# Three recurrent layers and an attention: the scan's blocks of four rounds, five of them passes of one loop, become three blocks of 16, 16 and 4 rounds written out

## The chip, the cores and the metric

The kernel runs on one core of a Trainium2 chip, in float32. The metric is the time of one execution on the device in microseconds (us), as the median of three runs. TensorE does the matmuls, VectorE (DVE in the profile), ScalarE (ACT) and GpSimd (POOL) the elementwise work, SyncE (SP) issues transfers. Each engine runs its own stream of instructions; they meet at semaphores.

## The reference

The input x holds 8 sequences of 512 time steps and 512 features, cond is the first state of each. Three recurrent layers and one causal attention are each added to x in turn:

```
_L0: step(h, x_t):
        fused = sigmoid(concatenate([x_t, h]) @ w_W + w_b)
        hidden_state, output_state = split(fused, 2)
        memory_state = x_t @ wx_W + wx_b + hidden_state * (h @ wh_W + wh_b)
        h_new = output_state * h + (1.0 - output_state) * tanh(memory_state)
_L1, _L2: xw = x @ Wx + b
        step(h_prev, xw_t): h_next = tanh(xw_t + h_prev @ Wh)
_L3: causal multi-head attention (16 heads of 32) over x, with one more key and value from cond

x = x + _L0(x, cond)
x = x + _L1(x, cond)
x = x + _L2(x, cond)
x = x + _L3(x, cond)
```

The scans are serial in time: 512 steps, each with matmuls of an 8-row state with 512x512 weights. What does not hang on the state (x_t times a weight) can be computed for many time steps at once.

## The kernel before

All of x lies in SBUF as X. Time is cut into chunks of 16 steps (CH), 32 in all (NCH). The scan goes by rounds of 16 steps: in round m, layer 0 runs over chunk m, layer 1 over chunk m - 2 and layer 2 over chunk m - 4, so that all three run at the same time, shifted. With the shift there are 36 rounds (ROUNDS). From round 4 to round 31 all three layers run in each; rounds 0 and 1 hold layer 0 alone, and rounds 32 to 35 only the rest of layers 1 and 2.

One step of a full round, on TensorE: 16 matmuls (32 records in the trace) for the reset gate and the candidate of layer 0 (L181, into ps0), 16 for its update gate (L187), 16 for layers 1 and 2 together (L201, `main12`), and then the "fills": one or two groups of 16 matmuls (L225) that multiply a staged chunk with an input weight, for the steps of the next round. The 20 fills of a full round are spread over its 16 steps, two of them in every fourth step. VectorE turns the results (L328, L335 and L269), adds the input products, gates, and writes the new state h0 (L356); ScalarE does the sigmoids and tanh (L250, L253, L256, and L237, which writes the state h12). VectorE copies each finished fill out of PSUM with its bias (`keep_fills`, L290). Once a round and layer VectorE adds a finished chunk of states to X (L309), and GpSimd copies the next chunk of X to the staging tile of its layer (L381). `plan(m)` says what a round holds.

Within a block the streams are written out in full. `scan_rounds` makes one block of four rounds (PER_BLOCK): it calls `scan_block` and then `clear_signals`, a barrier of all engines that sets the semaphores to zero, so that a block counts from zero again. All waits in a block are for numbers counted from its start (`n0`, `n12`, `nfill`, `nchunk`). Before and after the streams of a block each engine branches (L171 and L150 in TensorE's listing). The blocks begin at rounds 0, 4, 8, 28 and 32; the one at round 8 (RAMP) is the body of a loop, `nc.Fori` at L106, that runs five times, for the rounds 8 to 27. Inside it the chunk of X is addressed through a register (`bass.ds(i * ...)` in `x_chunk`). At the end of each pass each engine adds to its register, compares, and branches back.

Only the first block (`first == 0`) loads the input and state weights of layers 1 and 2; in it each fill of these layers waits for the weights besides its other waits. The block from round 32 on (`first >= NCH`) loads the weights of the attention. After the scan come the last chunk's add, the attention's setup and `attention_batches`, a loop of two passes over four sequences each. These are the same before and after.

Of the kernel before, what the change touches and what calls it, by code (L numbers as in the profile page):

```python
# [28 lines left out]
CH = 16  # L29
NCH = T // CH  # L30
N = CH * B
ROUNDS = NCH + 4
G0 = 3 * KC
XW = G0 + KC
SLOTS = 2
PER_BLOCK = 4
RAMP = 8


BIAS_ROWS = [("w_b", 8), ("wh_b", 4), ("wx_b", 4), ("b1", 4), ("b2", 4),  # L40
# [9 lines left out]
def fills_of(m):  # L50

    out = []
    if -1 <= m < NCH - 1:
        out += [(0, g) for g in range(G0)]
    if 0 <= m - 1 < NCH:
        out += [(1, g) for g in range(KC)]
    if 0 <= m - 3 < NCH:
        out += [(2, g) for g in range(KC)]
    return out


def plan(m):


    fills = fills_of(m)
    n = len(fills)

    late = 0 if m < NCH - 1 else 3
    by_step = [[]] * late + [fills[n * s // (CH - late):n * (s + 1) // (CH - late)] for s in range(CH - late)]
    chunk_ops = [[] for _ in range(CH)]  # L70
    if m < NCH - 1:
        chunk_ops[0].append(("stage", 0, m + 1))
    at = 1
    for layer, c in ((1, m - 1), (2, m - 3)):
        if 0 <= c < NCH:
            chunk_ops[at].append(("add", layer - 1, c))
            chunk_ops[at + 1].append(("stage", layer, c))
        at += 2
    if 0 <= m - 5 < NCH:
        chunk_ops[at].append(("add", 2, m - 5))  # L80
    layers = [l for l, c in ((0, m - 2), (1, m - 4)) if 0 <= c < NCH]
    return {"scan0": 0 <= m < NCH, "scan12": layers, "fills": by_step, "chunk_ops": chunk_ops}
# [6 lines left out]
def clear_signals(nc, mem):  # L89

    nc.all_engine_barrier(sems_to_clear=mem.sem_range)
# [5 lines left out]
    return rows.rearrange("p g (q j r) -> p j g q r", q=KC, j=KC)[:, j]  # L97


def scan_rounds(nc, mem, sems, a, first, times):  # L100

    plans = [plan(first + u) for u in range(PER_BLOCK)]
    steps = [(u, t) for u in range(PER_BLOCK) for t in range(CH)]
    S = len(steps)
    if times > 1:
        with nc.Fori(0, times) as i:  # L106
            scan_block(nc, mem, sems, a, plans, steps, S, first, i)
            clear_signals(nc, mem)
    else:
        scan_block(nc, mem, sems, a, plans, steps, S, first, None)  # L110
        clear_signals(nc, mem)


def scan_block(nc, mem, sems, a, plans, steps, S, first, i):
    s = sems
    X, stage, h0, h12, xw0, xw12 = mem.X, mem.stage, mem.h0, mem.h12, mem.xw0, mem.xw12

# [32 lines left out]
    with nc.Block(no_gpsimd_drain=True) as block:  # L150
# [80 lines left out]
        def _(act):  # L231
            def tanh12(n, u, t):
                act.wait_ge(s.pre12, n12[n] + 1)

                ls = plans[u]["scan12"]
                l0, l1 = ls[0], ls[-1] + 1
                nc.scalar.activation(h12[:, u % 2, :, t, l0:l1, :].rearrange("p k l b -> p l k b"), mem.sum12[:, l0:l1, :, :],  # L237
                                     ACT.Tanh).then_inc(s.h12_new, 1)
# [20 lines left out]
            if plans[u]["scan12"]:  # L259
                tanh12(S - 1, u, t)  # L260

        @block.vector
        def _(dve):
            def pre12(n, u, t):

                ls = plans[u]["scan12"]
                l0, l1 = ls[0], ls[-1] + 1
                dve.wait_ge(s.main12_done, n12[n] + 1)
                nc.vector.transpose(mem.tp12[:, P * l0:P * l1], mem.ps12[:, P * l0:P * l1]).then_inc(s.turned12, 1)  # L269
                dve.wait_ge(s.turned12, n12[n] + 1)  # L270
                apart = P + B if len(ls) == 2 else P
                nc.vector.tensor_tensor(  # L272
                    mem.sum12[:, l0:l1, :, :],
                    mem.tp12[:, 0:2 * apart].rearrange("p (l x) -> p l x", l=2)[:, l0:l1, 0:P]
                    .rearrange("p l (q c) -> p l q c", q=KC)[:, :, :, 0:B],
                    xw12[:, u % 2, l0:l1, :, t, :], ALU.add).then_inc(s.pre12, 1)

            def keep_fills(n, u, t):

                if plans[u]["fills"][t]:  # L280
                    dve.wait_ge(s.fill_done, nfill[n + 1])
                for f, (layer, g) in enumerate(plans[u]["fills"][t]):
                    if layer == 0:
                        at = g if g < 2 * KC else g + KC
                        dst = xw0[:, 1 - u % 2, at, :, :]
                        bias = BIAS_AT["w_b"] + g if g < 2 * KC else BIAS_AT["wx_b"] + g - 2 * KC
                    else:
                        dst = xw12[:, 1 - u % 2, layer - 1, g, :, :]
                        bias = BIAS_AT[f"b{layer}"] + g
                    nc.vector.tensor_scalar(  # L290
                        dst, mem.fillps[n % 2][:, f * N:(f + 1) * N].rearrange("p (t b) -> p t b", b=B),
                        mem.biasT[:, bias:bias + 1], None, ALU.add).then_inc(s.fill_kept, 1)

            def x_chunk(c):

                if i is None:
                    return X[:, :, :, c * CH:(c + 1) * CH]
                return X[:, :, :, bass.ds(i * (PER_BLOCK * CH) + c * CH, CH)]

            def chunk_adds(n, u, t):  # L300

# [56 lines left out]
            u, t = steps[-1]  # L358
            if plans[u]["scan12"]:
                pre12(S - 1, u, t)  # L360
            keep_fills(S - 1, u, t)

        @block.gpsimd
        def _(pool):
            def x_chunk(c):

                if i is None:
                    return X[:, :, :, c * CH:(c + 1) * CH]
                return X[:, :, :, bass.ds(i * (PER_BLOCK * CH) + c * CH, CH)]

            done = 0
            for n, (u, t) in enumerate(steps):
                p = plans[u]
                for kind, layer, c in p["chunk_ops"][t]:
                    if kind == "stage":

                        if done:
                            pool.wait_ge(s.chunk_op, done)
                        if u and (u - 1, layer) in last_fill:
                            pool.wait_ge(s.fill_done, last_fill[u - 1, layer])  # L380
                        nc.gpsimd.tensor_copy(  # L381
                            stage[layer][:, :, :].rearrange("p k (t b) -> p k b t", b=B),
                            x_chunk(c)).then_inc(s.chunk_op, 1)
                    done += 1
# [723 lines left out]
def build(nc, a, out):  # L1108
    mem = Mem()
    with ExitStack() as ctx:  # L1110
        def sb(stack, name, shape):
            return stack.enter_context(nc.sbuf_tensor(name, shape, F32))
# [4 lines left out]
        sems = Signals(lambda name: ctx.enter_context(nc.semaphore(name)))  # L1117
# [23 lines left out]
        with ExitStack() as scan:  # L1141
            mem.h0 = sb(scan, "h0", [P, SLOTS, KC, CH, B])
            mem.h12 = sb(scan, "h12", [P, SLOTS, KC, CH, 2, B])
            mem.wx = [mem.w_qkv, sb(scan, "wx1", [P, KC, D]), sb(scan, "wx2", [P, KC, D])]
            mem.wh12 = sb(scan, "wh12", [P, 2, KC, D])
            mem.xw0 = sb(scan, "xw0", [P, SLOTS, XW, CH, B])
            mem.xw12 = sb(scan, "xw12", [P, SLOTS, 2, KC, CH, B])
            mem.stage = [sb(scan, f"stage{l}", [P, KC, N]) for l in range(3)]
            mem.tp0 = sb(scan, "tp0", [P, G0 // KC * P])
            mem.tp12 = sb(scan, "tp12", [P, 2 * (P + B)])  # L1150
            mem.pre0 = sb(scan, "pre0_sb", [P, G0, B])
            mem.gates0 = sb(scan, "gates0_sb", [P, 2 * KC, B])
            mem.gated0 = sb(scan, "gated0_sb", [P, KC, B])
            mem.mem0 = sb(scan, "mem0", [P, KC, B])
            mem.tanh0 = sb(scan, "tanh0_sb", [P, KC, B])
            mem.held0 = sb(scan, "held0", [P, KC, B])
            mem.fresh0 = sb(scan, "fresh0_sb", [P, KC, B])
            mem.sum12 = sb(scan, "sum12", [P, 2, KC, B])
            with ExitStack() as load:
                mem.xrows = sb(load, "xrows", [P, 4, D])  # L1160
                mem.bias_rows = sb(load, "bias_rows", [P, P])
                mem.cond_rows = sb(load, "cond_rows", [P, D])
                setup(nc, mem, sems, a)
                clear_signals(nc, mem)
            m = 0
            while m < ROUNDS:
                times = (NCH - 1 - m) // PER_BLOCK if m == RAMP else 1
                scan_rounds(nc, mem, sems, a, m, times)
                m += PER_BLOCK * times
            add_last_chunk(nc, mem)  # L1170
            clear_signals(nc, mem)

# [76 lines left out]
```

## Time and profile before

| | |
|---|---|
| median of 3 runs | 4201.73 us |
| lowest and highest | 4198.7 and 4204.33 us |
| the profiled execution's own time | 4198.98 us |
| its span, first to last instruction | 4197.3 us |
| mean granted clock of TensorE | 0.975 |
| TensorE, matmul busy | 3891.2 us, 93% of the span |
| VectorE, ScalarE, GpSimd busy | 2455.8, 1057.7 and 126.9 us |

The page gives the busy time of each engine, its share in 40 slices of the span, and TensorE's granted clock in the same slices; the clock has two levels here, 1.2 and 2.4 GHz, given as 0.5 and 1 of full speed. The windows give the same for chosen stretches. The timeline gives runs of like instructions with their starts, and in brackets how long the engine had stood idle and what ended that. "issue" stands for a wait that no event in the profile explains, "PEq L91", "POOLq L91" and "SPq L150" for an engine's own queue at a barrier. The scan begins with the matmuls at 67.5 us and its last full round ends at about 2817; the attention begins at 3027.

### The profile page before, as it was taken

Reading aid. Unit: us, or ns where it says so; the run is one execution under the profiler, and the core shown is the slowest. Engines: PE = TensorE matmul, PEld = TensorE weight load, DVE = VectorE, ACT = ScalarE, POOL = GpSimd, SP = SyncE. Lnnn points to the kernel's source line nnn. Section 1 sums busy time; section 2 is a strip of 40 time slices with the busy share of each in tenths; the row PEclk is TensorE's granted clock in tenths of the full one; section 3 lists DMA queues with packets and bytes.
Section 4 is the critical chain, followed back from the end, with each engine's and each line's share of the span. In section 5 each row is a group of like instructions: output and inputs, shape, how many; then the busy total and the mean of one; then the engine's idle time right before and its main releaser. Section 6 shows DMA issues by size and latency. Waiting matters only on the chain. (4 is left out here: it accounts for less than half of the span.)

```text
span 4197.3 us, 167926 instructions
## 1 busy us (share of the span) xinstructions
PE 3891.2 (93%) x75946; PEld 2493.0 (59%) x75946; DVE 2455.8 (59%) x9312; ACT 1057.7 (25%) x3796; POOL 126.9 (3%) x137
## 2 busy tenths in 40 slices
PE   6799999999999999999999999997689888888988
PEld 5577777777666666666666667754444444444444
DVE  3565665665566556566656656653375667557565
ACT  1121111111111111111111111110053454345444
POOL 0000000000000000000000000000000000000000
PEclk9999999999999999999999999999799999999999
DMA  5000000000000000000000000010000000000000
GB/s 182 3 4 4 3 4 3 3 4 3 4 3 3 4 3 3 4 3 3 3 4 3 3 3 3 3 50 15 1 1 11 11 1 11 11 11 1 11 11 11
DMA packets 16600, 44.53 MB, mean 11 GB/s; under 512 B 1474, under 2 KB 1522, under 8 KB 15876
## 3 DMA queue, kind: packets, MB, share of 16 engines
q1 hardware_dynamic: 13572, 27.33, 1.8%
q8 instruction: 607, 9.95, 1.0%
q10 hardware_dynamic: 2304, 6.29, 0.4%
q14 instruction: 117, 0.96, 0.1%
HBM read 25.23 MB, written 8.39 MB: 8 GB/s over the span
## 5 line engine op out<-in xcount | busy, mean ns | idle before, releaser
L181 PE MATMUL bank<-wh,h 128*8 128x256 f32 x16384 | 983.8, 381 | 62.0 <-DVE h L356 31.4
L201 PE MATMUL bank<-wh,h 128*16 128x256 f32 (+1 forms) x17408 | 991.7, 369 | 52.8 <-ACT h L237 50.8
L201 PEld LDWEIGHTS bank<-wh,h 128*16 128x16 f32 (+1 forms) x17408 | 491.1, 97 | 372.0 <-ACT h L237 73.1
L181 PEld LDWEIGHTS bank<-wh,h 128*8 128x8 f32 x16384 | 434.2, 90 | 420.3 <-DVE h L356 50.3
L328 DVE STREAM_TRANSPOSE tp<-bank 128x256 f32<-128x256 f32 x512 | 230.4, 450 | 642.4 <-PE bank L181 642.4
L187 PE MATMUL bank<-wh,h 128*8 128x128 f32 x16384 | 542.3, 273 | 0.0
L187 PEld LDWEIGHTS bank<-wh,h 128*8 128x8 f32 x16384 | 434.7, 90 | 125.3 <-issue 2.0
L250 ACT ACTIVATE gates_sb<-pre_sb 128x32 f32<-128x32 f32 x512 | 118.2, 231 | 1355.6 <-DVE pre_sb L330 1355.6
L225 PE MATMUL bank<-stage,w_qkv 128*32 128x128 f32 x11904 | 382.2, 273 | 0.0
L225 PEld LDWEIGHTS bank<-stage,w_qkv 128*32 128x32 f32 x11904 | 335.7, 110 | 51.2
L269 DVE STREAM_TRANSPOSE tp<-bank 128x256 f32<-128x256 f32 (+1 forms) x544 | 236.1, 434 | 174.0 <-PE bank L201 113.1
L237 ACT ACTIVATE h<-sum 128x64 f32<-128x64 f32 (+1 forms) x544 | 138.4, 254 | 784.8 <-DVE sum L272 784.8
L290 DVE TENSOR_SCALAR xw<-bank,biasT 128x128 f32<-128x128 f32 x628 | 209.8, 349 | 174.9 <-PE bank L225 174.9
L719 PE MATMUL bank<-X,w_qkv 128*128 x512 | 254.3, 643 | 48.9 <-DVE image_scores L908 19.3
L845 ACT ACTIVATE probs<-probs,neg_max 128x385 f32<-128x385 f32 (+3 forms) x512 | 280.0, 549 | 0.0
L923 DVE CUSTOM_DVE_ANT_0 probs<-bank,addends 128x384 f32<-128x384 f32 (+3 forms) x512 | 220.3, 487 | 93.4 <-PE bank L732 92.8
L858 ACT COPY probsT<-bank 128x512 f32<-128x512 f32 (+1 forms) x352 | 177.9, 546 | 367.4 <-PE bank L750 366.0
L225 PE MATMUL bank<-stage,wx 128*32 128x128 f32 x8192 | 262.5, 274 | 0.0
L225 PEld LDWEIGHTS bank<-stage,wx 128*32 128x32 f32 x8192 | 233.0, 111 | 34.7
L750 PE MATMUL bank<-ident,probs 128*128 128x128 f32 x1280 | 194.7, 296 | 37.4 <-ACT probsT L858 24.6
L750 PEld LDWEIGHTS bank<-ident,probs 128*128 128x128 f32 x1280 | 154.1, 152 | 103.8 <-issue 45.6
L335 DVE STREAM_TRANSPOSE tp<-bank 128x128 f32<-128x128 f32 x512 | 162.2, 317 | 80.2 <-PE bank L187 75.3
(133 smaller groups left out, 3273.6 us busy)
## 6 DMA issues: line engine op xcount, KB each, us to landing
xrows<-in_x_dram SPq DMA_DIRECT2D x32, 256.0 KB, 3.8
out_dram<-probs SPq DMA_DIRECT2D x32, 256.0 KB, 2.0
w_qkv<-in_L_cond_c_attn_w_dram SPq DMA_DIRECT2D x1, 3072.0 KB, 18.2
wh<-in_L_cond_w_W_dram ACTq DMA_DIRECT2D x4, 512.0 KB, 8.2
w_qkv<-in_L_cond_w_W_dram ACTq DMA_DIRECT2D x4, 512.0 KB, 10.0
wx<-in_L_cond_Wx_dram SPq DMA_DIRECT2D x2, 1024.0 KB, 8.3
wh<-in_L_cond_Wh_dram SPq DMA_DIRECT2D x2, 1024.0 KB, 10.5
wh<-in_L_cond_wh_W_dram ACTq DMA_DIRECT2D x4, 256.0 KB, 8.6
```

Source lines behind the costliest of these rows:

```text
L181: mm = pe.matmul(mem.ps0[32 * j:32 * j + B, 0:2 * P], h0[:, us, k, ts, :], columns_of(mem.wh0[:, k, 0:3:2, :], j), start=(k == 0), stop=(k ...
L187: mm = pe.matmul(mem.ps0o[32 * j:32 * j + B, 0:P], h0[:, us, k, ts, :], columns_of(mem.wh0[:, k, 1:2, :], j), start=(k == 0), stop=(k == K ...
L201: mm = pe.matmul(mem.ps12[32 * j:32 * j + B * len(ls), P * l0:P * l1], h12[:, us, k, ts, l0:l1, :].rearrange("p l b -> p (l b)"), columns_ ...
L225: mm = pe.matmul(mem.fillps[n % 2][32 * j:32 * (j + 1), f * N:(f + 1) * N], w[:, k, at:at + 32], stage[layer][:, k, :], start=(k == 0), st ...
L269: nc.vector.transpose(mem.tp12[:, P * l0:P * l1], mem.ps12[:, P * l0:P * l1]).then_inc(s.turned12, 1)
L290: nc.vector.tensor_scalar(dst, mem.fillps[n % 2][:, f * N:(f + 1) * N].rearrange("p (t b) -> p t b", b=B), mem.biasT[:, bias:bias + 1], No ...
L328: nc.vector.transpose(mem.tp0[:, 0:2 * P], mem.ps0[:, 0:2 * P]).then_inc(s.turned0, 1)
L719: mm = pe.matmul(bank[:, :], mem.w_qkv[:, k, at:at + P], mem.X[:, k, batch(u), :].rearrange("p o t -> p (o t)"), start=(k == 0), stop=(k = ...
L750: mm = pe.transpose(bank[:, (h * n + kc) * P:(h * n + kc + 1) * P], mem.probs[:, v % RING, g, at:at + P], mem.ident[:, :])
L845: nc.scalar.activation(row, row, ACT.Exp, bias=mem.neg_max[:, i % RING, g:g + 1], accum_out=mem.sums[:, i % RING, g:g + 1]).then_inc(s.exp ...
L858: nc.scalar.copy(mem.probsT[:, per * r:per * (r + 1), 0:n, qc * P:(qc + 1) * P], bank[:, 0:per * n * P].rearrange("p (h k q) -> p h k q", ...
L923: nc.vector.tensor_tensor_reduce(out=mem.probs[:, slot, g, EXTRAS:EXTRAS + n], in0=mem.banks[g][:, 0:n], in1=mem.addends[:, TRI[qc]:TRI[qc ...
```

## The change

The rounds are cut at 0, 16 and 32 (BLOCKS), and each block is written out once: `scan_rounds` takes the number of rounds, the loop and the loop's register are gone, and `x_chunk` takes X by constants. `plan`, the order of instructions in a round and all tiles stay. The barrier with its clearing of semaphores stays behind each block. The first block, with its waits for the layer weights, now holds rounds 0 to 15.

```diff
-PER_BLOCK = 4
-RAMP = 8
+BLOCKS = [0, NCH // 2, NCH]
...
-def scan_rounds(nc, mem, sems, a, first, times):
-
-    plans = [plan(first + u) for u in range(PER_BLOCK)]
-    steps = [(u, t) for u in range(PER_BLOCK) for t in range(CH)]
-    S = len(steps)
-    if times > 1:
-        with nc.Fori(0, times) as i:
-            scan_block(nc, mem, sems, a, plans, steps, S, first, i)
-            clear_signals(nc, mem)
-    else:
-        scan_block(nc, mem, sems, a, plans, steps, S, first, None)
-        clear_signals(nc, mem)
...
+def scan_rounds(nc, mem, sems, a, first, rounds):
+
+    plans = [plan(first + u) for u in range(rounds)]
+    steps = [(u, t) for u in range(rounds) for t in range(CH)]
+    scan_block(nc, mem, sems, a, plans, steps, len(steps), first)
+    clear_signals(nc, mem)
...
-                if i is None:
-                    return X[:, :, :, c * CH:(c + 1) * CH]
-                return X[:, :, :, bass.ds(i * (PER_BLOCK * CH) + c * CH, CH)]
+                return X[:, :, :, c * CH:(c + 1) * CH]
...
-            m = 0
-            while m < ROUNDS:
-                times = (NCH - 1 - m) // PER_BLOCK if m == RAMP else 1
-                scan_rounds(nc, mem, sems, a, m, times)
-                m += PER_BLOCK * times
+            for first, last in zip(BLOCKS, BLOCKS[1:] + [ROUNDS]):
+                scan_rounds(nc, mem, sems, a, first, last - first)
```

TensorE before, at the end of the loop's body: the last step of its fourth round (rounds 11, 15, 19, 23 and 27), the end of the loop, and the block that follows it in the code, of round 28. For rounds 11 to 23 the row COMPARE_AND_BRANCH leads back to the head of the body.

```order
740 L181 MATMUL bank<-wh,h 8x256 x16
741 L187 MATMUL bank<-wh,h 8x128 x16
742 L201 MATMUL bank<-wh,h 16x256 x16
743 L225 MATMUL bank<-stage,wx 32x128 x32
744 L150 UNCONDITIONAL_BRANCH
745 L106 REGISTER_ALU
746 L106 COMPARE_AND_BRANCH
747 L171 UNCONDITIONAL_BRANCH
748 L181 MATMUL bank<-wh,h 8x256 x16
749 L187 MATMUL bank<-wh,h 8x128 x16
```

TensorE after, at one of these places, from round 11 to round 12 (the lines have moved: L174, L180, L194 and L218 are L181, L187, L201 and L225 of before).

```order
735 L174 MATMUL bank<-wh,h 8x256 x16
736 L180 MATMUL bank<-wh,h 8x128 x16
737 L194 MATMUL bank<-wh,h 16x256 x16
738 L218 MATMUL bank<-stage,wx 32x128 x32
739 L174 MATMUL bank<-wh,h 8x256 x16
740 L180 MATMUL bank<-wh,h 8x128 x16
741 L194 MATMUL bank<-wh,h 16x256 x16
742 L218 MATMUL bank<-stage,w_qkv 32x128 x16
```

The matmuls of the two rounds now follow each other directly, without barrier, register or branch. From round 15 to round 16 TensorE after has the one boundary inside the full rounds; it has the form of those that before went straight on.

```order
993 L194 MATMUL bank<-wh,h 16x256 x16
994 L218 MATMUL bank<-stage,wx 32x128 x32
995 L143 UNCONDITIONAL_BRANCH
996 L164 UNCONDITIONAL_BRANCH
997 L174 MATMUL bank<-wh,h 8x256 x16
998 L180 MATMUL bank<-wh,h 8x128 x16
```

GpSimd before, at the block of rounds 4 to 7 (its 12 copies) and the loop's head, where each copy has a register instruction (ISA) ahead of it.

```order
17 L363 UNCONDITIONAL_BRANCH
18 L381 COPY stage<-X 128x4x8x16 x12
19 L150 UNCONDITIONAL_BRANCH
20 L91 ISA
21 L106 UNCONDITIONAL_BRANCH
22 L363 UNCONDITIONAL_BRANCH
23 L381 ISA
24 L381 COPY stage<-X 128x4x8x16
25 L381 ISA
```

GpSimd after, the whole scan up to the block of round 32.

```order
13 L354 UNCONDITIONAL_BRANCH
14 L370 COPY stage<-X 128x4x8x16 x44
15 L143 UNCONDITIONAL_BRANCH
16 L90 ISA
17 L354 UNCONDITIONAL_BRANCH
18 L370 COPY stage<-X 128x4x8x16 x47
```

The copies of sixteen rounds stand in a row, without register instructions.

## Rows read from the trace of the kernel before

**Rows 1.** The page: span, busy time and the larger queue of instructions.

```profile
span 4197.3 us, 167926 instructions
...
PE 3891.2 (93%) x75946; PEld 2493.0 (59%) x75946; DVE 2455.8 (59%) x9312; ACT 1057.7 (25%) x3796; POOL 126.9 (3%) x137
...
q8 instruction: 607, 9.95, 1.0%
```

**Rows 2.** Windows, columns in their first line: from block to block, one round, behind a jump.

```profile
core 0: us, PE busy (x) PEld busy (x) DVE busy (x) ACT busy (x) POOL busy (x), PEclk, DMA share, GB/s
67.50:361.74 294.24, 260.59 (x7168) 191.10 (x7169) 166.05 (x708) 52.92 (x225) 8.96 (x8) 1.00 0.05 18
361.74:711.00 349.26, 346.96 (x8704) 250.44 (x8705) 210.31 (x795) 60.83 (x256) 13.66 (x12) 1.00 0.01 3
711.00:1063.37 352.37, 346.96 (x8704) 249.58 (x8704) 211.46 (x796) 60.84 (x256) 14.78 (x13) 1.00 0.01 3
1063.37:1418.37 355.00, 349.07 (x8704) 228.35 (x8704) 211.38 (x796) 60.80 (x256) 13.87 (x12) 0.99 0.01 3
1418.37:1773.12 354.75, 349.06 (x8704) 228.42 (x8704) 211.39 (x796) 60.80 (x256) 13.86 (x12) 0.99 0.01 3
1773.12:2127.72 354.60, 349.18 (x8704) 228.46 (x8704) 211.36 (x796) 60.86 (x256) 13.83 (x12) 0.99 0.01 3
2127.72:2479.21 351.49, 349.37 (x8704) 233.73 (x8705) 211.44 (x796) 60.84 (x256) 12.85 (x12) 0.99 0.01 3
...
797.70:884.40 86.70, 86.70 (x2184) 62.42 (x2180) 53.00 (x199) 15.22 (x64) 3.42 (x3) 1.00 0.01 3
1063.40:1069.00 5.60, 5.60 (x84) 2.75 (x88) 1.29 (x5) 0.30 (x2) 0.00 (x0) 0.61 0.03 7
```

**Rows 3.** Timeline of one step in the loop: start, duration, engine, instructions.

```profile
802.92 1.92 PE L181 MATMUL bank<-wh,h 128*8 128x256 f32 x32
...
807.17 0.19 DVE L356 TENSOR_TENSOR h<-held,fresh_sb 128x32 f32<-128x32 f32 x1
...
808.12 1.92 PE L181 MATMUL bank<-wh,h 128*8 128x256 f32 x32
```

**Rows 4.** Waits of TensorE in the scan: us in total, times, longest.

```profile
PE bank L181 <- issue: 22.4, 4, 5.9
PE bank L181 <- PEq L91: 8.2, 4, 2.3
```

**Rows 5.** Timeline of GpSimd: staging copy of layer 0 in successive rounds.

```profile
851.91 1.14 POOL L381 COPY stage<-X 128x512 f32 x1 [35.74 <-PE bank L225]
...
938.60 1.14 POOL L381 COPY stage<-X 128x512 f32 x1 [35.83 <-PE bank L225]
```

**Rows 6.** Timeline at the boundary behind round 7.

```profile
708.79 0.61 DVE L290 TENSOR_SCALAR xw<-bank,biasT 128x128 f32<-128x128 f32 x2 [1.04 <-PE bank L225]
...
711.03 1.91 PE L181 MATMUL bank<-wh,h 128*8 128x256 f32 x32 [2.30 <-PEq L91]
```

**Rows 7.** Timeline of TensorE's weight loads at the boundary behind round 3.

```profile
357.45 1.77 PEld L225 LDWEIGHTS bank<-stage,wx 128*32 128x32 f32 x64
361.74 1.23 PEld L181 LDWEIGHTS bank<-wh,h 128*8 128x8 f32 x28 [2.52 <-issue]
```

**Rows 8.** Timeline where the loop begins anew, behind round 11 (last row: 23).

```profile
1060.19 1.10 POOL L381 COPY stage<-X 128x512 f32 x1 [70.73 <-SPq L150]
...
1063.37 3.60 PE L181 MATMUL bank<-wh,h 128*8 128x256 f32 x32 [5.38 <-issue]
...
2127.72 3.60 PE L181 MATMUL bank<-wh,h 128*8 128x256 f32 x32 [5.42 <-issue]
```

**Rows 9.** Windows, the rest of the scan and the attention.

```profile
2814.00:3000.00 186.00, 127.19 (x2651) 76.48 (x2643) 54.90 (x171) 16.53 (x68) 7.87 (x14) 0.90 0.10 36
3000.00:4197.30 1197.30, 1035.63 (x5437) 537.43 (x5435) 743.75 (x2843) 552.77 (x1698) 12.18 (x24) 0.94 0.02 8
```

**Rows 10.** Timeline of GpSimd: the second sequence in each pass of the attention.

```profile
3121.22 0.40 POOL L1022 COPY k_image_b<-k_image 128x16 f32 x1 [92.40 <-PE bank L704]
...
3708.27 0.40 POOL L1022 COPY k_image_b<-k_image 128x16 f32 x1 [96.07 <-PE bank L704]
```

More of the change, by code:

```diff
@@ L97, in columns_of, with scan_block @@
     return rows.rearrange("p g (q j r) -> p j g q r", q=KC, j=KC)[:, j]
-def scan_rounds(nc, mem, sems, a, first, times):
-    plans = [plan(first + u) for u in range(PER_BLOCK)]
-    steps = [(u, t) for u in range(PER_BLOCK) for t in range(CH)]
-    S = len(steps)
-    if times > 1:
-        with nc.Fori(0, times) as i:
-            scan_block(nc, mem, sems, a, plans, steps, S, first, i)
-            clear_signals(nc, mem)
-    else:
-        scan_block(nc, mem, sems, a, plans, steps, S, first, None)
-        clear_signals(nc, mem)
-def scan_block(nc, mem, sems, a, plans, steps, S, first, i):
+def scan_rounds(nc, mem, sems, a, first, rounds):
[3 more added lines that the diff above has]
+    clear_signals(nc, mem)
+def scan_block(nc, mem, sems, a, plans, steps, S, first):
     s = sems
@@ L365, in x_chunk @@
             def x_chunk(c):
-                if i is None:
-                    return X[:, :, :, c * CH:(c + 1) * CH]
-                return X[:, :, :, bass.ds(i * (PER_BLOCK * CH) + c * CH, CH)]
+                return X[:, :, :, c * CH:(c + 1) * CH]
             done = 0
```

## The prediction

> **What bounds the kernel now.** I read the page first, then the windows from block to block, then the timelines of the places that the change touches. The page [rows 1] says that TensorE is busy for 93% of the span. The windows [rows 2] say it sharper. A stretch of one round inside a block, 86.70 us long, has 86.70 us of matmul and a granted clock of 1.00. The timeline of one step [rows 3] shows why: its first group of matmuls (L181) starts at 802.92, and after the update gate (L187), the two simple layers (L201) and an input product (L225) the next step starts at 808.12, a step of 5.20 us. The state that the next step needs was written at 807.17 and took 0.19 us, so it was there some 0.75 us before TensorE could use it. In these rounds VectorE, ScalarE and GpSimd have slack, and TensorE sets the pace, step by step, at its full rate.
>
> So what the change can give back there is only time in which TensorE stands still or runs slowly. That happens in one kind of place: where one block ends and another begins. The first four rounds are another matter: their window from 67.50 to 361.74 has 33.65 us without a matmul [rows 2], nearly all of it waits for the state, as there the chain of one step is longer than its matmuls, and that stays. The other waits of TensorE in the scan [rows 4] are 22.4 us in 4 pieces of up to 5.9 us that end by "issue", and 8.2 us in 4 pieces of up to 2.3 us that end by "PEq L91", the release of the barrier.
>
> **The yardstick.** A round with no boundary in it lasts 86.69 us: GpSimd's staging copy of layer 0, which waits each round for the same matmul group of TensorE, starts at 851.91 in one and at 938.60 in the next [rows 5]. Four rounds without a boundary are thus 346.76 us.
>
> **The change part by part.** Before, the scan's 36 rounds stand in nine blocks of four, five of which are passes of one loop; after, in three blocks. The boundaries behind rounds 3, 7 and 27 (straight on into other code) go, those behind rounds 11, 19 and 23 (back to the head of the loop) go, the one behind round 15 becomes one that goes straight on, and the one behind round 31 stays as it is.
>
> *A boundary that goes straight on.* Behind round 7 VectorE starts at 708.79 to copy the last two input products out of PSUM; then all engines meet, the semaphores are cleared, and TensorE starts at 711.03 after 2.30 us of idle time [rows 6]. The whole window from round 4 to round 8 is 349.26 us [rows 2], 2.50 over the yardstick. Without the boundary the copies lie beside the next step's matmuls, as in every other round, and TensorE has its next operand 0.75 us early, so all 2.50 go. Behind round 3 the weight loads of the last fill start at 357.45 and take 1.77, to 359.22, and the next block's begin at 361.74 after 2.52 [rows 7]: 2.50 again. The boundary behind round 27 is one more of the four pieces of up to 2.3 us [rows 4]. (The fourth stands ahead of round 0, and isn't touched.)
>
> *A boundary that goes back.* Behind round 11 the barrier is over when GpSimd's first copy starts, at 1060.19. But TensorE starts only at 1063.37, 3.18 us later and 5.38 us after its last matmul, and then needs 3.60 us [rows 8] for a group that elsewhere takes 1.92 [rows 3]. The granted clock of that stretch is 0.61, so much of it lies at the lower of its two levels, 1.2 GHz and not 2.4 [rows 2]. So a jump back costs about 3 us more idle time than a straight boundary, and 2 us of slow matmuls after it. The other three look alike: the last has 5.42 us idle and a group of 3.60 again [rows 8], the four together 22.4 [rows 4]. After the boundary with 2.30 us of idle time the group takes 1.91, full rate [rows 6].
>
> *The sum.* The six windows from 361.74 to 2479.21 [rows 2] are 349.26, 352.37, 355.00, 354.75, 354.60 and 351.49 us, over the yardstick by 2.50, 5.61, 8.24, 7.99, 7.84 and 4.73: together 36.91 us for the boundaries behind rounds 7, 11, 15, 19, 23 and 27. (Of it about 4.9 us are the two straight ones, so 32.0 are the four jumps back, 8.0 each: 5.5 more than a straight one.) Add 2.50 for round 3, take off 2.50 for the straight boundary that now stands behind round 15: **36.9 us saved**. The profiled execution took 4198.98 us for its 4197.3 of span; it would go to 4162.1. From the median of 4201.73 it gives 4164.8.
>
> *Registers.* In the loop the adds of VectorE and the copies of GpSimd take their place in X from a register. GpSimd's copy takes 1.14 us with the register [rows 5] in a round that is all matmul, and neither engine is waited for: nothing. *An added wait.* The first block waits for the layer weights before each input product of layers 1 and 2; it now holds 16 rounds and not 4, so some 96 more products carry that wait, long satisfied. The last two products of round 3 both carry it, and their 64 weight loads run through as one piece of 1.77 us [rows 7], 28 ns a load: nothing. *Earlier copies.* At rounds 4, 8 and so on GpSimd may copy the next chunk in the middle of the round before, not behind the barrier. It does so in all other rounds, under the same full matmul rate. *Instruction fetch.* The loop saves no fetching that I could lose: 9.95 MB came over the larger of the two instruction queues for 167926 instructions [rows 1], about 59 bytes for each one executed, so each pass of the loop was fetched anew. The straight stretches of up to four rounds show no stall inside.
>
> The Trainium skill bears on the jump: its page "Runtime: NRT & Kernel Launch", section "Instruction fetch mechanics", says that fetching ahead is purely sequential, and that a taken branch to a target outside the small window held must fetch it first. The 5.38 us behind the jumps back agree with it.
>
> **After the scan** nothing is changed, but it begins 37 us earlier. There the clock falls now and then: 0.90 over 186 us and 0.94 over 1197 us [rows 9], which is 37 and 144 us at the lower level. Where these pieces fall against the matmuls can shift. The attention's second pass repeats the first (its second sequence begins at 3121.22 and again at 3708.27, 587.05 us later [rows 10]) as a copy of it. If a twentieth of the low time, 9 us, came or went, that would be 4.5 us of time. With the 2.8 us by which the three runs differ from their median I take plus or minus 7.
>
> **The rivals.**
> (a) *The jump's price stays at the boundaries that are left.* Block ends are branches too, and the code before them is now four times as long. If TensorE's fetch missed behind rounds 15 and 31 as it does at a jump back, each would cost 5.5 us more: 11 us, 4175.8 us. Against it: no straight boundary in the trace idles over 2.52 us [rows 4, 7], though four rounds of 8704 matmuls stand before each, and that is already too long for a jump back over them to go without a pause. The rule of the skill named above would allow it only if the next block's code doesn't follow directly. 6 in 100.
> (b) *The barrier was a cover.* If the copies and adds that the barriers held together made TensorE wait in other steps once they are gone, the straight boundaries' share (2.50 three times) would come back: 4172.3 us. Against it, the window of rounds 4 to 7 holds three round changes, and of its 349.26 us all but the 2.30 of its end are matmul (346.96) [rows 2]. 4 in 100.
> (c) *Slower: the clock.* TensorE would now run for about 1334 us and then for about 1378 us with only one short pause between. If so long a load made the granted clock fall, each us at the lower level would cost half a us of matmul, and from 74 us at that level on the change loses. At 100 us at that level it is 4164.8 + 50 = 4215 us. Against it: the windows from 67.50 to 1063.37 have 1.00 with pauses of 2.5 us only, and in the scan's full rounds 0.99 stands only in windows that hold or begin with a jump's pause. 2 in 100.
> (d) *It doesn't do what it says*, that is, code is still shared or barriers remain. The order of instructions excludes it: each engine's scan has three stretches. 0. That the tail gives back nearly all of the gain by its clock phase, leaving the time within 0.2%: 3 in 100, at about 4195 us.
>
> **How the numbers follow.** The forecast, 4165 us (0.991 of before), has 85 in 100. Its own range is 4158 to 4172; with half of (a) and (b) I give 4156 to 4175. A measurement of this kernel can tell 0.2%, 8.4 us, from no change; the forecast is over four times that. Faster 0.95, the same 0.03, slower 0.02.
>
> **What would show it.** In the profile after: round 4 begins 2.5 us earlier than 361.74, round 8 about 5.0 earlier than 711.00, and from there to round 16 the rounds follow at 86.69 us, where 1063.37 and 1418.37 stood; waits of TensorE by "issue" of 5 us are gone from the scan; one pause of 2.3 us stands just ahead of 1402, with a full-rate group behind it; the granted clock is 1.00 from the first round to round 31. (a) would show a pause over 5 us there and a group of 3.60 behind it; (b) PE waits at round changes; (c) a clock below 1.00 in mid-round. I would be wrong if the tail behind 2814 changes its length by more than a few us.

## The result and the profile after

| | before | after |
|---|---|---|
| median | 4200.22 us (4 runs, 4195.46 to 4204.33) | 4161.65 us (4 runs, 4159.03 to 4164.38) |
| the profiled execution's own time | 4198.98 us | 4159.44 us |
| its span | 4197.3 us | 4157.7 us |
| mean granted clock | 0.975 | 0.978 |

The ratio is 0.9909, with a 95% interval of 0.9891 to 0.9926: 38.6 us less, where 36.9 were forecast. The time lies 3.4 us below the forecast of 4165.

The windows of the kernel after answer to [rows 2]. They begin at the first weight load of rounds 0, 4, 8, 16 and 31; one more is a single round, and one is all that follows.

```profile
core 0: us, PE busy (x) PEld busy (x) DVE busy (x) ACT busy (x) POOL busy (x), PEclk, DMA share, GB/s
65.12:356.67 291.55, 260.22 (x7165) 191.04 (x7169) 164.54 (x706) 52.58 (x225) 10.22 (x9) 1.00 0.05 18
356.67:703.44 346.77, 346.77 (x8713) 242.82 (x8708) 209.66 (x795) 60.47 (x257) 13.53 (x12) 1.00 0.01 3
703.44:1399.09 695.65, 693.83 (x17420) 485.65 (x17412) 421.94 (x1594) 120.87 (x512) 25.94 (x24) 1.00 0.01 3
1399.09:2699.41 1300.32, 1300.29 (x32637) 936.07 (x32641) 791.02 (x2983) 226.67 (x960) 51.40 (x45) 1.00 0.01 3
790.00:876.70 86.70, 86.70 (x2184) 60.71 (x2180) 52.68 (x199) 15.11 (x64) 3.38 (x3) 1.00 0.01 3
2699.41:4157.70 1458.29, 1239.24 (x9809) 659.83 (x9800) 845.12 (x3190) 583.34 (x1826) 22.36 (x40) 0.94 0.03 11
```

Rounds 4 to 7 take 346.77 us, the yardstick to a hundredth, and all of it is matmul: the 2.50 us that the boundary cost in [rows 2] are gone and nothing has come in their place. Rounds 8 to 15 take 695.65, which is eight rounds of 86.69 and 2.13 for the one boundary that is left. (From matmul to matmul it is 2.03: in mid-stream a round's weight load starts 0.10 us ahead of its matmul, behind a pause 0.03.) Rounds 16 to 30 are 1300.32, or 15 times 86.69, without a pause and at clock 1.00. The first four rounds, 291.55 and not 294.24, lost their boundary only; the rest was the chain of their steps.

The waits of TensorE in the scan answer to [rows 4]. The first column is the total, then how many, then the longest.

```profile
PE bank L174 <- DVE h L347: 31.3, 32, 1.7
PE bank L174 <- PEq L90: 3.4, 2, 1.8
PE bank L194 <- PEq L90: 1.6, 1, 1.6
```

No wait ends by "issue" any more (22.4 us in 4 pieces before). Two by the barrier are left ahead of L174, at round 0 and round 16, and one ahead of L194 at round 32. This is the timeline of the one behind round 15:

```profile
1397.34 0.61 DVE L283 TENSOR_SCALAR xw<-bank,biasT 128x128 f32<-128x128 f32 x2 [1.04 <-PE bank L218]
...
1399.12 1.91 PE L174 MATMUL bank<-wh,h 128*8 128x256 f32 x32 [1.84 <-PEq L90]
```

Here a jump back had cost 8.2 us. Now the barrier leaves 1.84 us of idle time, and the group behind it runs at the full rate.

From the first group of the scan to that of round 31 the kernel before took 2671.7 us (67.5 to 2739.2) and the kernel after 2634.3 (65.1 to 2699.4): 37.4 us. Everything behind that took 1458.12 before and 1458.29 after. The remaining 2.4 us of the 39.5 by which the two profiled executions differ lie ahead of the scan, which began at 67.5 and at 65.1; no instruction there is changed, and over the executions of this study its begin wanders from 64.0 to 69.1.

### The profile page after: what moved, and what is told of

Read it like the earlier page. It is cut to its first block and busy times, and to the rows that moved or that the text cites. A ratio compares the mean times of both kernels' runs of the same rounds, so it can differ in the third digit from the quotient of the medians.

```text
span 4157.7 us, 167702 instructions
## 1 busy us (share of the span) xinstructions
PE 3880.4 (93%) x75946; PEld 2546.0 (61%) x75946; DVE 2451.1 (59%) x9312; ACT 1054.6 (25%) x3796; POOL 126.2 (3%) x137
## 3 DMA queue, kind: packets, MB, share of 16 engines
q8 instruction: 600, 9.83, 1.0%
## 5 line engine op out<-in xcount | busy, mean ns | idle before, releaser
L194 PE MATMUL bank<-wh,h 128*16 128x256 f32 (+1 forms) x17408 | 1002.4, 372 | 52.3 <-ACT h L230 50.7
L174 PE MATMUL bank<-wh,h 128*8 128x256 f32 x16384 | 979.7, 379 | 34.7 <-DVE h L347 31.3
L194 PEld LDWEIGHTS bank<-wh,h 128*16 128x16 f32 (+1 forms) x17408 | 512.4, 97 | 358.7 <-ACT h L230 75.7
L174 PEld LDWEIGHTS bank<-wh,h 128*8 128x8 f32 x16384 | 454.3, 90 | 369.4 <-DVE h L347 50.1
L180 PE MATMUL bank<-wh,h 128*8 128x128 f32 x16384 | 542.7, 273 | 0.0
L180 PEld LDWEIGHTS bank<-wh,h 128*8 128x8 f32 x16384 | 451.2, 90 | 105.2
L218 PE MATMUL bank<-stage,w_qkv 128*32 128x128 f32 x11904 | 383.8, 273 | 0.0
L218 PEld LDWEIGHTS bank<-stage,w_qkv 128*32 128x32 f32 x11904 | 339.1, 110 | 47.9
L218 PE MATMUL bank<-stage,wx 128*32 128x128 f32 x8192 | 262.5, 274 | 0.0
L218 PEld LDWEIGHTS bank<-stage,wx 128*32 128x32 f32 x8192 | 234.2, 111 | 32.6
L739 PE MATMUL bank<-ident,probs 128*128 128x128 f32 x1280 | 194.3, 294 | 37.4 <-ACT probsT L847 24.8
```

Of the source, the lines that this page charges most:

```text
L174: mm = pe.matmul(mem.ps0[32 * j:32 * j + B, 0:2 * P], h0[:, us, k, ts, :], columns_of(mem.wh0[:, k, 0:3:2, :], j), start=(k == 0), stop=(k ...
L180: mm = pe.matmul(mem.ps0o[32 * j:32 * j + B, 0:P], h0[:, us, k, ts, :], columns_of(mem.wh0[:, k, 1:2, :], j), start=(k == 0), stop=(k == K ...
L194: mm = pe.matmul(mem.ps12[32 * j:32 * j + B * len(ls), P * l0:P * l1], h12[:, us, k, ts, l0:l1, :].rearrange("p l b -> p (l b)"), columns_ ...
L218: mm = pe.matmul(mem.fillps[n % 2][32 * j:32 * (j + 1), f * N:(f + 1) * N], w[:, k, at:at + 32], stage[layer][:, k, :], start=(k == 0), st ...
L739: mm = pe.transpose(bank[:, (h * n + kc) * P:(h * n + kc + 1) * P], mem.probs[:, v % RING, g, at:at + P], mem.ident[:, :])
```

## Experiments

Where a run has several executions, the time is their median, compared with executions of the kernel before on the same chip; four runs have a single execution, and of these the trace is read. "The scan" is from the first group of round 0 to that of round 31, in the profile.

**Without the jump, with all barriers.**

```diff
-BLOCKS = [0, NCH // 2, NCH]
+BLOCKS = list(range(0, ROUNDS, 4))
```

> The scan is written out, but its barriers stay after every four rounds: nine blocks, eight boundaries, all straight. This is the removal of the loop alone. Theory (a jump back costs 8.0 us, a straight boundary 2.5): the four jumps save 5.5 each, 22 us, so 4200.2 - 22 = 4178 us; the windows of four rounds are all 349.2 to 349.3 us, no pause of TensorE over 2.5 us and a full-rate group behind each. Rival (the 8 us belong to the barrier and the clearing of semaphores inside the full rounds, not to the jump): the boundaries behind rounds 11 to 23 stay near 8 us, and the time near 4200.

Measured: 4177.89 us (4172.39 to 4178.7), ratio 0.9945 (0.9929 to 0.9962). The scan takes 2647.5 us, 24.2 less than before. The timeline behind round 11, where [rows 8] show 5.38 us and 3.60:

```profile
1054.90 1.94 PE L218 MATMUL bank<-stage,wx 128*32 128x128 f32 x64
1058.66 1.92 PE L174 MATMUL bank<-wh,h 128*8 128x256 f32 x32 [1.82 <-PEq L90]
```

So the jump and not the barrier had cost most: with the same barriers at the same places 23 of the 38.6 us are back. The four boundaries inside the former loop leave 1.82 us of idle time, not the 2.30 taken from round 7; each costs 2.0 us against none, not 2.5. Hence 24 and not 22. Of the 6.0 us that a jump costs more than these boundaries, 3.8 are idle time and 2.2 slow matmuls.

The listing of the loop's line in the kernel before shows where the added idle time lies: in the branch itself. These are its rows behind round 11; for each engine's queue they give the duration in ns (three times the same, as there is one row) and the start in us.

```profile
L106 POOLq COMPARE_BRANCH  x1: 45/45/45, 1059.8 to 1059.8; - x1
...
L106 PEldq COMPARE_BRANCH  x1: 3356/3356/3356, 1060.0 to 1060.0; - x1
L106 POOLq MOVE  x1: 34/34/34, 1060.0 to 1060.0; - x1
L106 DVEq MOVE  x1: 43/43/43, 1063.0 to 1063.0; - x1
```

TensorE's branch lasts 3.36 us (up to 3.88 in the other passes). Behind round 27, where it isn't taken, it is short:

```profile
L106 PEldq COMPARE_BRANCH  x1: 79/79/79, 2479.1 to 2479.1; - x1
```

VectorE, whose body is long too, stands for 3.0 us between its branch at 1059.9 and its next instruction. GpSimd jumps back at the same moment over a dozen copies and goes on at once. That fits a fetch of the jump's target, which the long streams need and the short one doesn't; the barrier is the same for all three.

**A body of two rounds: nine jumps in place of four.**

```diff
+LOOPED = 2
...
-                times = (NCH - 1 - m) // PER_BLOCK if m == RAMP else 1
-                scan_rounds(nc, mem, sems, a, m, times)
-                m += PER_BLOCK * times
+                times = 20 // LOOPED if m == RAMP else 1
+                rounds = LOOPED if m == RAMP else PER_BLOCK
+                scan_rounds(nc, mem, sems, a, m, times, rounds)
+                m += rounds * times
```

> The kernel before with a loop body of two rounds and ten passes for rounds 8 to 27: nine jumps back and not four, and everything else as before. Theory (each jump back costs 8.0 us in all, whatever the body's length as long as it is thousands of instructions): five more jumps at places where no boundary was, + 40 us, 4240 us. Rival (the cost goes with the length of the body, fetched anew over it): nine jumps of 4 us, 36 against 32 us, 4204 us.

Measured: 4236.78 us (4232.08 to 4239.1), ratio 1.0088 (1.0071 to 1.0104), 35.5 us over the kernel before. The scan grew by 39.8 us; in the profiled executions the part behind it was 3.2 us shorter (1454.9 and 1458.1). The waits of TensorE in it:

```profile
PE bank L182 <- issue: 50.0, 9, 5.9
...
PE bank L182 <- PEq L92: 8.2, 4, 2.3
```

Nine pieces of 5.6 us on average, as the four of before (22.4 / 4 = 5.6): the price goes by the jump, not by what is jumped over. Each jump costs 7.4 to 7.9 us with its slow group. The timeline shows a surprise at two places where nothing jumps: entering the loop, and behind it.

```profile
711.52 2.69 PE L182 MATMUL bank<-wh,h 128*8 128x256 f32 x32 [2.31 <-PEq L92]
...
2517.86 3.36 PE L182 MATMUL bank<-wh,h 128*8 128x256 f32 x32 [2.11 <-PEq L92]
```

After pauses of 2.31 and 2.11 us these groups took 2.69 and 3.36 us, not 1.91. In the kernel before, a pause of 2.30 at the same boundary had a full-rate group behind it [rows 6]. Each of the two cost 1.7 us, so 3.4 of the 39.8 us are not the jumps': the five added ones brought 7.3 each and not 8.

**A body of ten rounds: one jump.** The same edit with `LOOPED = 10`.

> The kernel before with a loop body of ten rounds and two passes for rounds 8 to 27: one jump back and not four. Theory (8 us for each jump, independent of the body's length): 4201 - 24 = 4177 us, the same as the written-out scan with blocks of four, which has no jump but four more straight boundaries of 2.1 us: 8 against 8.4. Rival (the longer body makes the jump dearer): the pause behind round 17 is clearly over 5.9 us.

Measured: 4174.54 us (4173.4 to 4178.03), ratio 0.9933 (0.9916 to 0.9949). The one jump, over ten rounds:

```profile
1585.44 3.60 PE L182 MATMUL bank<-wh,h 128*8 128x256 f32 x32 [5.76 <-issue]
```

The pause is 5.76 us, and those of the body of two rounds, a fifth as long, are 5.36 to 5.85 us: length plays no part between 2 and 10 rounds. With its slow group the jump costs 7.8 us. The scan takes 2649.0 us, 22.7 less than before for three jumps fewer. It keeps the registers, so the gain of the written-out blocks wasn't theirs. Here too the group behind round 7 was slow, after 2.30 us.

**Pauses without a jump.** Straight blocks of four, and at the end of a block:

```diff
+PAUSES = {0: 2, 4: 3, 8: 4, 12: 5, 16: 6, 20: 7, 24: 8}
...
+            if first in PAUSES:
+                pool.wait_ge(s.fill_done, nfill[S])
+                for q in range(PAUSES[first]):
+                    nc.gpsimd.memset(mem.scratch[:, 512 * (q % 2):512 * (q % 2) + 512], 0.0).then_inc(s.wide_zero, 1)
+                    pool.wait_ge(s.wide_zero, q + 1)
```

> Straight blocks of four rounds as in the run with straight boundaries only, but at the end of each block up to round 27 GpSimd clears a scratch tile 2, 3, 4, 5, 6, 7 and 8 times (some 0.5 to 0.6 us each) after the last matmul, so that TensorE's pauses grow from about 2.4 to about 6 us without any jump. The scratch tile is used for nothing. Theory (the lower clock behind a jump comes from the length of the pause): the short pauses are followed by a group of 1.91 us, the long ones, at 5.4 us at the latest, by one of 3.60 us and 2 us of loss. Rival (the slow matmuls come from the fetch behind the jump, which delivers them slowly): all groups take 1.91 us whatever the pause.

Measured: one execution, 4199.59 us. The first group behind four of the seven boundaries; where the rows end inside it, it has fewer than 32 records:

```profile
362.45 1.91 PE L175 MATMUL bank<-wh,h 128*8 128x256 f32 x32 [2.85 <-PEq L91]
...
712.38 3.17 PE L175 MATMUL bank<-wh,h 128*8 128x256 f32 x28 [2.97 <-PEq L91]
...
1417.06 3.17 PE L175 MATMUL bank<-wh,h 128*8 128x256 f32 x28 [4.15 <-PEq L91]
...
2124.89 3.60 PE L175 MATMUL bank<-wh,h 128*8 128x256 f32 x32 [5.31 <-PEq L91]
```

After 5.31 us without a jump the group takes 3.60 us, just as after the 5.38 us of a jump. So slow matmuls behind a jump need no slow fetch of them: the fetch makes the pause long, and a pause of that length is enough to lower the clock. The windows of the steps behind the pauses of 2.97 and 6.22 us have a granted clock of 0.75 and 0.72:

```profile
712.30:719.20 6.90, 6.82 (x128) 4.09 (x132) 2.54 (x11) 0.69 (x3) 1.12 (x1) 0.75 0.01 2
2480.00:2487.00 7.00, 6.95 (x124) 3.97 (x128) 2.48 (x10) 0.69 (x3) 1.12 (x1) 0.72 0.01 4
```

All six pauses of 2.97 to 6.22 us were followed by slow groups, the one of 2.85 was not. The loss did not grow steadily with the pause: the first step took 6.48 us after a pause of 4.73 and 7.81 after one of 4.15, where 5.20 is usual.

**Seven pauses just above the usual.** The same, with two clearings at each boundary.

> As e3_pauses, but with two clearings of the scratch tile at each of the seven boundaries, which gave a pause of 2.85 us and a full-rate group in the one case seen. Theory (between the pauses of 1.8 to 2.3 us, which nearly never lower the clock, and those of 3.5 us and more, which did each time, it is a matter of chance): some of the seven groups are slow, some not. Rival (a pause of 2.85 us is safe): all seven take 1.9 us.

Measured: one execution, 4187.26 us. The pauses came out at 2.39 to 2.85 us. Two of those of 2.39:

```profile
1416.61 1.91 PE L175 MATMUL bank<-wh,h 128*8 128x256 f32 x32 [2.39 <-PEq L91]
...
1765.96 3.48 PE L175 MATMUL bank<-wh,h 128*8 128x256 f32 x32 [2.39 <-PEq L91]
```

Six of the seven groups were slow; the one behind round 15 was not, after the same 2.39 us as the next. So the length alone does not decide in this range; what does is not shown. The step that begins with a slow group takes 6.60 to 6.88 us where 5.20 is usual, 1.4 to 1.7 us lost.

**The body of two rounds again.** The kernel of e2_loop2, unchanged.

> The loop body of two rounds once more, unchanged, for a second look. In the first look two pauses without a jump (2.31 us behind round 7, and 2.1 us behind round 27) were followed by a first group at the lower clock (6.8 us to the next step and not 5.1). If that hangs on the code at these places, it comes again at both; if it hangs on where in time the pause falls, it can be absent at one or both. The jumps' pauses are followed by slow groups all nine times in either case.

Measured: one execution, 4236.21 us. The groups behind rounds 7 and 27 were slow again, as were those behind all nine jumps, and now the one behind round 3 too, which in e2_loop2 was not. These two rows are of the same place of the same program, the first from e2_loop2:

```profile
362.25 1.91 PE L182 MATMUL bank<-wh,h 128*8 128x256 f32 x32 [2.28 <-PEq L92]
```

and the second from this run:

```profile
360.61 3.53 PE L182 MATMUL bank<-wh,h 128*8 128x256 f32 x32 [2.28 <-PEq L92]
```

Same code, same pause, 1.6 us apart in time, and another clock. The code alone does not decide it.

**Many short pauses.** `BLOCKS = list(range(0, ROUNDS, 2))`, 17 straight boundaries; the attention's weights are loaded in the block of round 32 alone.

> The written-out scan with a barrier after every two rounds: 18 blocks, 17 boundaries, all straight, nine more than with blocks of four. Against e1_straight4 (4177.9 us, 2.1 us for most boundaries): if a pause of 2.1 us never lowers the clock, 4178 + 9 x 2.1 = 4197 us. In e2_loop2 two pauses of 2.1 and 2.3 us were followed by slow matmuls at the lower clock; if that is chance of place and happens at a third of the boundaries, some 5 of 17 groups behind a boundary take over 1.92 us, with 1.6 us of loss for each: 4205 us.

Measured: 4191.9 us (7 runs, 4185.74 to 4197.69), ratio 0.9974 (0.9962 to 0.9986). The waits of TensorE in the scan:

```profile
PE bank L174 <- PEq L90: 29.4, 16, 2.2
```

16 pauses of 1.84 us on average, the one ahead of round 0 among them. None of the 14 behind rounds 3 to 29 (1.82 to 1.91 us) lowered the clock. The one behind round 1 did, after 2.19 us: its group took 3.35 us. In the full rounds each boundary costs 2.0 us of scan, and the scan is 15.5 us longer than with blocks of four. The expectation of 18.9 took 2.1 us for all nine added boundaries. One of them, behind round 33, lies behind what is called the scan here; and those behind rounds 7 and 27 are 0.3 us shorter than with blocks of four. The part behind the scan took 1466.2 us in the profiled execution, so the total says little about single boundaries.

**One block.** `BLOCKS = [0]`, with the attention's weights loaded behind two waits in place of the barrier.

```diff
-BLOCKS = [0, NCH // 2, NCH]
+BLOCKS = [0]
...
-        if first >= NCH:
+        if first == 0:
...
+                sp.wait_ge(s.update_done, n0[S])
+                sp.wait_ge(s.fill_done, last_fill[NCH - 2, 0])
```

> The whole scan in one block: the two boundaries that the changed kernel kept (2.1 us of extra time behind round 15 and about 2 behind round 31) go as well; the attention's weights are loaded when layer 0's last matmul and last input product are done. Theory: 4 us less than the changed kernel, 4157.5 us. Rival (the scan's end is bounded by the loading of the attention's weights, or fetching suffers over so long a stretch): no gain, 4161 us or more, with a pause of TensorE behind round 31 or in the rounds.

Measured: 4158.2 us (4155.56 to 4159.58), ratio 0.9901 (0.9884 to 0.9917). The scan takes 2632.3 us, 2.0 less than after. The time fits the expected 4157.5; by the runs' spread alone it can't be told from the changed kernel, but the trace can: all waits by the barrier inside the scan are gone, and over 36 rounds in a row no fetch stalls.

**The attention's passes written out as well,** on top of the one block.

```diff
-        with nc.Fori(0, B // BATCHES) as part:
+        for part in range(B // BATCHES):
```

> The whole scan in one block, and the attention's two passes written out as well, with its barrier kept between them. The pause of TensorE there was 9.99 us before (to 3614.45). Theory (the fetch behind a jump back costs TensorE 3.3 us more than the barrier alone): 3.3 us less than e4_one_block, 4155 us, with a pause of about 6.7 us. Rival (that pause ends by the last output rows and their transfers, not by the fetch): the pause stays near 10 us, 4158 us.

Measured: 4157.19 us (4152.96 to 4162.13), ratio 0.9887 (0.987 to 0.9903). TensorE's pause between the passes, in e4_one_block with the jump:

```profile
3573.75 6.65 PE L710 MATMUL bank<-X,w_qkv 128*128 x8 [9.50 <-issue]
```

and here:

```profile
3576.83 5.83 PE L710 MATMUL bank<-X,w_qkv 128*128 128x512 f32 x8 [5.21 <-PEq L90]
```

The pause is 4.3 us shorter (3.3 expected): a jump's fetch costs the same sort of sum here. In the median 1.0 us of it arrived, within the spread. In the profiled execution, the slowest of the four, the part from round 31 on took longer all the same, 1462.06 us where e4_one_block took 1457.56:

```profile
2698.34:4160.40 1462.06, 1250.13 (x9809) 665.38 (x9800) 846.32 (x3190) 581.33 (x1825) 21.40 (x40) 0.93 0.03 11
```

The same 9809 records are busy for 1250.13 us, where they took 1239.71 in e4_one_block, at a clock of 0.93 and not 0.94: stretches at the lower clock took back more than the jump had given. This version has the lowest median, but whether it beats the one block is open.

**The changed kernel again.**

> The changed kernel unchanged, for a second look at its one boundary inside the full rounds and at the time behind the scan. Theory: the scan from its first group to round 31 takes 2634.3 us as before, or 1.6 us more if the clock falls behind round 15; whatever else differs lies behind the scan, in the stretches at the lower clock.

Measured: one execution, 4161.39 us. The scan took 2634.35 us (2634.29 in the first profile of this kernel), the rest 1458.12 (1458.29), and the scan began 2.1 us later (67.2 and 65.1). The scan is the same to 0.1 us; the difference lies ahead of it.

## Why the prediction was right

- *TensorE's matmuls set the pace of the full rounds.* Right. Inside the blocks its windows are filled to 100% in both kernels, and a round without a boundary takes 86.69 us in each. Each us of idle time that went out of them went out of the total.
- *The sum.* Forecast 36.9 us, measured 37.4 in the scan. The difference has a place: the boundary kept behind round 15 was sized by the one behind round 7 at 2.50 us, and cost 2.0 (1.84 us idle, not 2.30). The boundaries that went were read from their own windows and were right. The rest of the 38.6 us, between medians, lies ahead of the scan and in the runs' spread.
- *Why the boundaries of 1.82 and of 2.1 to 2.3 us differ* is known in part. In e1_straight4 those behind rounds 3, 7 and 27 are the longer ones and those between the shorter, with the same instructions on TensorE; with blocks of two all three are short. The extra time lies in the queues of other engines at the barrier. Behind round 3 VectorE's drain comes 0.3 us after TensorE's and takes 0.14 us where 0.02 is usual:

```profile
L90 PEldq DRAIN  x1: 13/13/13, 359.6 to 359.6; - x1
L90 DVEq DRAIN  x1: 136/136/136, 359.9 to 359.9; - x1
```

  Behind round 27 it is ScalarE's drain, and behind round 7 GpSimd's queue stands for 0.38 us between clearing the semaphores and its next instruction, where 0.03 is usual. What held them stays open.
- *A jump back costs 5.5 us more than a straight boundary.* Shown, by taking the jumps alone away (24.2 us for four, 6.0 each against the short boundaries) and by adding five. Its two parts were read rightly: more idle time, and then slow matmuls. That such a pause is enough for the second, without a slow fetch, only the pauses without a jump showed. The Trainium skill's page "Runtime: NRT & Kernel Launch", section "Instruction fetch mechanics", has the first part: a taken branch to a target outside the window held must fetch it before anything goes on. TensorE's branch rows of 3.36 to 3.88 us agree.
- *Registers, the added wait for the weights, earlier copies: nothing.* Right. Rounds 4 to 15 of after carry the added wait, rounds 16 to 30 don't, and both take 86.69 us a round, as did the rounds with registers in the loop before.
- *(a) The jump's price stays at the kept boundaries.* No: 1.84 us idle and a group of 1.91, and 1.6 us idle behind round 31. (The 8704 that the prediction calls matmuls are records of the trace, two for each matmul here.)
- *(b) The barrier was a cover.* No: rounds 4 to 7 are 346.77 us of matmul in 346.77.
- *(c) The clock under long load.* No: 1.00 over rounds 16 to 30, and in e4_one_block the whole scan has no stretch at the lower level.
- *The part after the scan.* The forecast gave it room of a few us; it moved by 0.2 us in the two profiled executions. But over the variants that leave its code as it is, it ran from 1454.9 (e2_loop2) to 1461.8 us (e1_straight4), so the room was needed.
- One thing was taken as sure and was in part luck: a full-rate group behind the kept boundary, sized at 2.30 us of idle time. In the kernel before pauses of 2.1 to 2.3 us left the clock alone, three times in three; over all runs those of 2.1 to 2.9 us lowered it 13 times in 24. The kept boundary came out shorter, at 1.84 us, where it never fell. Had it fallen, the kernel would have been some 1.7 us slower, inside the range.

## What to carry to other kernels

Where one engine is full between barriers, the price of the barriers can be read off by comparing the repeating window with and without one, and their removal adds up. A loop on the engines costs one jump for each pass, here 7.4 to 8.2 us where a straight barrier costs 2.0 to 2.5, for bodies of 2, 4 and 10 rounds alike: write the loop out, or make its body long (one jump in place of four brought 0.7% of this kernel). No run here has a loop whose body is short on TensorE; GpSimd's jump back over its dozen copies cost it nothing that can be seen. And a pause of TensorE is to be counted with the slow matmuls that may follow it.

## What the runs showed of the hardware

- A jump back makes TensorE stand still for 5.4 to 5.9 us with the barrier in it, against 1.8 to 2.3 us for the barrier alone, for bodies of 2, 4 and 10 rounds alike. In the kernel before TensorE's branch row lasts 3.36 to 3.88 us when taken and 0.08 when not; GpSimd's, over a dozen copies, 0.04 either way.
- Pauses of TensorE at the boundaries behind rounds 1 to 29, and the clock behind them: 1.8 to 1.9 us, never lowered (none of 20: 14 with blocks of two, four in e1_straight4, and one in each of the two executions of the kernel after); 2.1 to 2.9 us, lowered or not, even at the same place of the same program (13 of 24 over all runs: six of seven in e10_pauses_285, none of three in the kernel before); 2.97 us and more, always lowered (all six in e3_pauses, and behind all 23 jumps of the scans). After a shorter pause the loss is 1.4 to 1.7 us, after a longer one 1.3 to 2.6. The Trainium skill's page "TensorE: Matmul & The Clock Gate", section "HAM oscillation — how this bites in real kernels", puts its rule against idle gaps at longer ones than these 2.1 to 3.0 us; here the measurement goes against it.
- Instruction fetching kept up with TensorE over the whole scan of 36 rounds written out: no wait in the scan of e4_one_block ends by "issue". The larger queue brought 9.95 MB of instructions before [rows 1] and 9.83 MB after. The loop saved no fetching.

```profile
q8 instruction: 600, 9.83, 1.0%
```
